# Self-attention: the narrow score parts of both heads share a bank and one maximum

## What is computed

```python
def _L1_attn_ref(x, wq, wk, wv, wo):
    NUM_HEADS = 16
    N, L, E = x.shape
    H, d = NUM_HEADS, E // NUM_HEADS
    q = (x @ wq.T).reshape(N, H, L, d)
    k = (x @ wk.T).reshape(N, H, L, d)
    v = (x @ wv.T).reshape(N, H, L, d)
    scores = jnp.einsum('nhld,nhmd->nhlm', q, k) / jnp.sqrt(jnp.float32(d))
    causal = jnp.tril(jnp.ones((L, L), dtype=bool))
    scores = jnp.where(causal, scores, jnp.float32(-jnp.inf))
    attn = jax.nn.softmax(scores, axis=-1)
    wei = jnp.einsum('nhlm,nhmd->nhld', attn, v).reshape(N, L, H * d)
    return wei @ wo.T
```

## Time and profile before

| | us |
|---|---|
| median of 3 runs (lowest, highest) | 3203.89 (3202.26, 3206.14) |
| the profiled execution, device time | 3204.56 |
| its span, first to last instruction | 3203.0 |
| of it self-attention's tiles, about | 1335 to 2108 |

### The profile page before, as it was taken

One profiled execution on the slowest core, in us unless ns is written; L12 is line 12 of the kernel. 1 busy time (PEld: TensorE's weight loads), 2 busy tenths in 40 slices (PEclk: granted clock), 3 DMA queues, 4 the chain that ended last, 5 costly groups with the idle time before them and its releaser, 6 DMA issues. The chain is left out here.

```text
span 3203.0 us, 41427 instructions
## 1 busy us (share of the span) xinstructions
PE 2843.9 (89%) x14210; PEld 1845.6 (58%) x14210; DVE 2080.0 (65%) x3833; ACT 1471.0 (46%) x2768; POOL 1509.9 (47%) x1192
## 2 busy tenths in 40 slices
PE   6898998998977877899999999978877999999998
PEld 2343343343333664555555555546666888888887
DVE  7899999999998654677777777758863222222221
ACT  5667667666763301366666656545541111111111
POOL 5788788888785553133333333256752111111111
PEclk8999999999999788899999999999888999999999
DMA  7135145145140162212322222110115665556662
GB/s 233 51 108 159 46 116 160 35 125 159 34 136 1 41 211 94 81 42 65 81 63 65 58 50 64 50 59 29 50 63 198 200 203 183 181 181 187 205 199 60
DMA packets 283856, 346.32 MB, mean 108 GB/s; under 512 B 85788, under 2 KB 238552, under 8 KB 283592
## 3 DMA queue, kind: packets, MB, share of 16 engines
q1 hardware_dynamic: 260399, 310.17, 31.3%
q0 software_dynamic: 16704, 27.21, 3.6%
q10 hardware_dynamic: 6544, 6.30, 0.7%
HBM read 234.69 MB, written 107.95 MB: 107 GB/s over the span
## 5 line engine op out<-in xcount | busy, mean ns | idle before, releaser
L542 POOL TENSOR_TENSOR mb_drive<-mb_dtx,mb_b_rep 128x1024 f32<-128x1024 f32 x255 | 597.0, 2355 | 179.9 <-DVE mb_pD L439 87.9
L853 PE MATMUL mb_pY<-mb_hc,ident 128*128 128x512 f32 x1024 | 502.9, 616 | 55.9 <-DVE mb_hc L456 55.5
L1981 DVE TENSOR_REDUCE at_nm_of<-at_pS 128x1 f32<-128x128 f32 (+1 forms) x756 | 401.6, 556 | 135.8 <-PE at_pS L1969 75.8
L3153 POOL DMA_INDIRECT out<-et_y,et_to x71 | 112.0, 1577 | 667.0 <-DVE et_y L3207 411.0
L3197 DVE TENSOR_TENSOR et_mT<-et_silu,et_pU 128x512 f32<-128x512 f32 (+1 forms) x160 | 100.3, 628 | 471.2 <-ACT et_silu L3168 471.1
L3168 ACT ACTIVATE et_silu<-et_pG 128x512 f32<-128x512 f32 (+1 forms) x160 | 87.8, 549 | 658.0 <-PE et_pU L3229 658.0
L853 PEld LDWEIGHTS mb_pY<-mb_hc,ident 128*128 128x128 f32 x1024 | 190.3, 195 | 326.9 <-issue 183.3
L1969 PE MATMUL at_pS<-at_kT,at_qT 128*128 128x128 f32 (+1 forms) x756 | 306.3, 407 | 65.3 <-DVE at_nm_of L1981 53.4
L598 ACT ACTIVATE mb_pD<-mb_dt,mb_a_neg 128x512 f32<-128x512 f32 x384 | 259.6, 688 | 157.3 <-DVE mb_hc L456 146.0
L439 DVE TENSOR_TENSOR_SCAN mb_pD<-mb_pD,mb_drive 128x1024 f32<-128x1024 f32 x128 | 292.7, 2287 | 42.9 <-ACT mb_pD L596 40.2
L445 DVE TENSOR_TENSOR_SCAN mb_pD<-mb_pD,mb_carried,mb_drive 128x512 f32<-128x512 f32 x256 | 314.0, 1271 | 6.8 <-ACT mb_pD L598 6.8
(11 more groups left out here) (491 smaller groups left out, 4984.7 us busy)
## 6 DMA issues: line engine op xcount, KB each, us to landing
t_wg<-in_t_wgT SPq DMA_DIRECT2D x40, 1024.0 KB, 6.3
t_wu<-in_t_wuT SPq DMA_DIRECT2D x40, 1024.0 KB, 8.8
t_wd<-in_t_wdT SPq DMA_DIRECT2D x40, 1024.0 KB, 11.3
mb_b_rep<-mb_rows SPq DMA_DIRECT2D x64, 512.0 KB, 5.6
mb_c_rep<-mb_rows SPq DMA_DIRECT2D x64, 512.0 KB, 4.8
t_h_sorted<-blank SPq DMA_DIRECT2D x6, 4160.0 KB, 20.2
t_h_sorted<-blank SPq DMA_DIRECT2D x18, 1170.0 KB, 6.2
t_h_sorted<-blank SPq DMA_DIRECT2D x12, 1040.0 KB, 5.8
```

Of the source, the lines that this page charges most:

```text
L542: nc.gpsimd.tensor_tensor(drive[G % RINGS][:, :, :], dtx[:, m, :].unsqueeze(1).to_broadcast([P, 2, CH]), b_rep[:, 2 * j:2 * j + 2, :], ALU ...
L853: last = nc.tensor.matmul(pY[:, :], K.ident[:, :], hc[G % RINGS][:, k, :], start=False, stop=(j == PAIRS - 1 and k == 1))
L1981: nc.vector.tensor_reduce(nm_of[t % 2][:, w0 // 512, a, qb:qb + 1], score_bank(t, k)[:, 0:w1 - w0], axis=AX.X, op=ALU.max, negate=True).th ...
```

## The change

A part of at most 256 keys becomes one unit for both sides: TensorE writes side 0 into the first columns of the bank and side 1 behind it, each with its mask, and signals once. VectorE reduces both with one instruction, which views the bank as two rows of keys and writes two maxima per query. Parts of 384 and 512 keys stay one unit per side. This gives 20 units (`NS`), and the groups' sizes become 3, 2, 2 at the head and 3, 2, 2, 2, 2, 2 for the rest. So `extra` has work only in g0 and g6. The same matmuls with the same shapes run as before. Only the grouping, the waits and their places in the order differ.

```diff
-        S_SIZES = [3, 3, 2, 3, 3, 3, 3, 2, 2]
-        S_ORDER = [(n, a) for n in range(NSP) for a in range(2)]
-        NS = len(S_ORDER)
+        S_SIZES = [3, 2, 2, 3, 2, 2, 2, 2, 2]
+        S_UNITS = []
+        for n, (qb, w0, w1) in enumerate(S_PARTS):
+            S_UNITS += [(n, [0, 1])] if w1 - w0 <= 256 else [(n, [0]), (n, [1])]
+        NS = len(S_UNITS)
...
-            last = nc.tensor.matmul(out[:, 0:w1 - w0], qT[b][:, a, h, qb * P:(qb + 1) * P], kT[b][:, a, h, w0:w1],
-                                    start=True, stop=not diag)
-            if diag:
-                last = nc.tensor.matmul(out[:, w1 - w0 - P:w1 - w0], ident_bf[:, :], after[:, :], start=False, stop=True)
+            for x, a in enumerate(sides):
+                last = nc.tensor.matmul(out[:, x * w:(x + 1) * w], qT[b][:, a, h, qb * P:(qb + 1) * P], kT[b][:, a, h, w0:w1],
+                                        start=True, stop=not diag)
+                if diag:
+                    last = nc.tensor.matmul(out[:, (x + 1) * w - P:(x + 1) * w], ident_bf[:, :], after[:, :], start=False, stop=True)
...
-            nc.vector.tensor_reduce(nm_of[t % 2][:, w0 // 512, a, qb:qb + 1], score_bank(t, k)[:, 0:w1 - w0], axis=AX.X,
+            nc.vector.tensor_reduce(nm_of[t % 2][:, w0 // 512, sides[0]:sides[0] + m, qb],
+                                    score_bank(t, k)[:, 0:m * w].rearrange("p (a w) -> p a w", a=m), axis=AX.X,
...
-                if nxt if g < 6 else far:
-                    pe_score(eng, i + ahead, x + ahead, pair, (S_AT[g + 3] if g < 6 else S_AT[g - 6]) + 2)
+                n = g + 3 if g < 6 else g - 6
+                if S_SIZES[n] > 2 and (nxt if g < 6 else far):
+                    pe_score(eng, i + ahead, x + ahead, pair, S_AT[n] + 2)
```

More of the change, by code:

```diff
@@ L1948, in score_bank, with pe_score @@
             return (pS + pE)[k % 4] if t == 0 else pS[k % 2]
-        def pe_score(eng, t, x, pair, k):
-            n, a = S_ORDER[k]
+        def pe_score(eng, t, tile, pair, k):
+            n, sides = S_UNITS[k]
             qb, w0, w1 = S_PARTS[n]
+            w = w1 - w0
             diag = w1 == (qb + 1) * P
-            b, h = x // 2 % 2, x % 2
+            b, h = tile // 2 % 2, tile % 2
             if k == 0 and h == 0:
@@ L1968, in pe_score @@
             out = score_bank(t, k)
-            last = nc.tensor.matmul(out[:, 0:w1 - w0], qT[b][:, a, h, qb * P:(qb + 1) * P], kT[b][:, a, h, w0:w1],
-                                    start=True, stop=not diag)
-            if diag:
-                last = nc.tensor.matmul(out[:, w1 - w0 - P:w1 - w0], ident_bf[:, :], after[:, :], start=False, stop=True)
+            for x, a in enumerate(sides):
[3 more added lines that the diff above has]
+                    last = nc.tensor.matmul(out[:, (x + 1) * w - P:(x + 1) * w], ident_bf[:, :], after[:, :], start=False, stop=True)
             last.then_inc(s_sc, 1)
         def dve_score(eng, t, k):
-            n, a = S_ORDER[k]
+            n, sides = S_UNITS[k]
             qb, w0, w1 = S_PARTS[n]
+            w, m = w1 - w0, len(sides)
             eng.wait_ge(s_sc, t * NS + k + 1)
@@ L2259, in scores @@
                 if nxt if g < 6 else far:
-                    base = S_AT[g + 3] if g < 6 else S_AT[g - 6]
-                    for k in range(base + lo, base + hi):
+                    n = g + 3 if g < 6 else g - 6
+                    base = S_AT[n]
+                    for k in range(base + lo, base + min(hi, S_SIZES[n])):
                         dve_score(eng, i + ahead, k)
```

## The result

The changed kernel takes 3154.75 us in the median (3152.41 to 3156.51, four executions) against 3203.07 us for the kernel before in the same session. The ratio is 0.9847, with a 95% interval of 0.983 to 0.9864: faster by 48 us, where 43 had been forecast.

A forecast was written before the change was run, and what follows sets the result against it. TensorE's stream sets the pace, losing time in pauses for VectorE's reduces. 14 tile pairs x (1.96 + 0.78) = 38.4 us, 42.5 with the other tiles, plus 0.3 at the first: profiled 3204.6 to 3161.7, forecast 3161 us, range 3156 to 3167.

The forecast's parts named there:

- the order for four engines: Hand-written walk through a tile's order, waits and durations; gave 21.34 us odd and 26.15 even for the kernel before.
- The saving on VectorE: Four fewer reduce instructions a tile, likelier 0.3 us of VectorE's time each tile; worth between nothing and 19 us.
- The even tile: Waits of 1.71, 1.37 and 0.5 us removed, 0.50 at v11 and 1.7 through ScalarE given back; net gain 1.96 us.
- The odd tile: Losses of 2.7 us removed in g0 to g4, 2.0 given back; with g6 and uncovered loads, a gain of 0.78 us.
- seven "losses": Odd tile, g0 to g4: seven delays of TensorE's score loads waiting for VectorE's reduces, adding up to 2.7 us.
- (b): Rival: more than the walk, a longer even-tile wait and g4's ScalarE waits go; 0.5 us more a pair, 3153 us; chance 0.12.
- The head: First tile: 20 units instead of 24 in VectorE's chain, saving 0.3 us for the four instructions.
- The maxima's way back: Row transfer of maxima to the next tile: cover falls from 1.4 to 1.5 us to 0.8, costing nothing.
- (a): Rival: ScalarE's chain takes nearly all the even tile's gain, leaving 0.82 us there; 24.5 us in all, 3179; chance 0.17.
- (c): Rival: the maxima come late by 1.2 us, each tile loses 0.4; 12 us less gain, 3173; chance 0.04.
- (d): Rival: waits reappear at the next bank, only 0.3 us of instruction overhead a tile saved; 10 us, 3194; chance 0.03.
- (e): Rival: coarser hand-over of merged units costs 1.6 us a tile; kernel slower by 7 us, 3211; chance 0.04.

The follow-up runs named there:

- e1: Changed kernel's order, but all 24 units keep their own bank, signal and reduce, narrow sides back to back; ratio to the kernel before 0.9958.
- e3: Kernel before, with VectorE reducing the third units of g1 and g3 ahead of the casts of turnings 3 and 7; ratio to before 0.9904.
- e4: Changed kernel, with its third units back in g1 and g3, behind VectorE's casts; ratio to the kernel before 0.9942.
- e6: Changed kernel with the third unit in g2 instead of g0; ratio to the kernel before 0.9835, odd tile 19.90 us.
- e7: Changed kernel with the casts of turning 5 made by VectorE instead of ScalarE; ratio to the kernel before 0.9806, even tile 23.48 us.
- e9: Changed kernel with only 128-key parts sharing a bank, 256-key parts two units again (22 units); one execution, 3166.7 us.
- e10: Changed kernel with the third unit in g2 and turning 5's casts on VectorE; one execution, 3158.2 us, even tile 24.31, odd 19.90.
- e2: Changed kernel with each merged unit reduced by two VectorE instructions, signalled after the second; ratio to the kernel before 0.9843.
- e8: Changed kernel with three useless small DMAs on SyncE ahead of the four carrying the maxima, a 1.32 us delay; one execution, 3185.5 us.

## Why the prediction was right, and where it was off

**The bound.** Right. TensorE's stream set the pace, and its waits for VectorE's reduces were the loss: as they went, the tiles shrank by about what the order for four engines had given, and none of e1, e3, e4, e6, e7, e9 and e10 came out more than 0.3 us a tile from what that order said of it.

**The saving on VectorE.** I left it between 0 and 19 us and put nothing of it into the tiles' sum. e2 shows the lower end: nothing. The two-row reduces cost what I had read from the earlier trace rows, 420 and 693 ns.

**The even tile.** Forecast 24.19, measured 24.23; but the gain was 2.17 us and not 1.96. What was taken away has the size forecast: the steps from load to load at the two pauses shrank from 1.82 to 0.23 us and from 1.61 to 0.11, together 3.09 where 3.08 stood in the sum, and that at the 384-key unit of g3 by 0.59 (0.5). The mis-sized term is what is given back. It was 0.52 us at v11 (0.50 forecast; it is loaded 2.80 us after the odd tile's start, 2.82 forecast), 0.20 + 0.19 at the two E of g4 (0.3), about 0.06 at product 0 (0.15), and at turning 7 only 0.51 us "more than before" (0.75): the wait is 0.78 us now, but 0.27 of it had been there. That makes 1.5 us instead of 1.7. ScalarE works without a gap, and e7 confirms its chain. The 0.27 may also be the 0.25 us by which my order for the tile before was short (26.15 against 26.40); that is not shown.

**The odd tile.** Forecast 20.56, measured 20.35, gain 1.00 and not 0.78. This came near in part by luck, for both sides of my sum were too large. One of the seven "losses" was none. It is the one at the third unit of g2, which follows product 0. The product's matmuls and that load in the kernel before, then the product in the changed one:

```profile
1718.88 1.07 PE L2093 MATMUL at_pO<-at_e,at_v 128*32 128x512 f32 x8
1719.88 0.19 PEld L1969 LDWEIGHTS at_pS<-at_kT,at_qT 128*128 128x128 f32 x1 [0.84 <-DVE at_nm_of L1981]
```

```profile
1698.09 1.06 PE L2099 MATMUL at_pO<-at_e,at_v 128*32 128x512 f32 x8
```

TensorE was busy with the product's matmuls for the whole 0.84 us, and the reduce that the load at 1719.88 needs had ended at 1718.77. Most likely this is what I counted with 0.76 us (1.00 less 0.24). In the same way the 0.84 us of idle time that the table puts down to ScalarE at 1699.08 lies under product 0 and is hardly a loss. Given back were 0.36 us at v9 (0.46 forecast), 0.52 at v11 (0.50), about 0.2 at product 0 (0.55; its load comes 0.71 us behind the one ahead, against 0.50 in the even tile before), and nothing in g4, where the 0.5 us did not appear. So about 1.1 us were given back, not 2.0, and about 2 taken away, not 2.7.

The places of the loads show where the gain arises: the first E of g3 comes 6.31 us after the tile's start in both kernels, and from there to g4's product the tile gains 0.99 us (9.68 to 8.69), where the kernel before had three waits of 0.52, 0.22 and 0.30 us for reduces. In g6, 0.66 us for the first unit (0.68), and none for the second (0.12).

**The sum.** 14 x 2.74 became 14 x 3.17; the median came out at 3154.75, 1.3 us below the forecast's own range and between it and rival (b). My own range, to which I had given 0.60, was missed by that little. (b) gave each pair 0.5 us more and 0.43 were measured, but not by its way: no wait that I had too short went away, and the waits for ScalarE in g4 are not covered in the even tile (0.39 us).

**The head.** Forecast -0.3 us, measured +1.1. VectorE's chain of 20 units did end 0.13 us sooner (from 1337.12 to 1350.05 against 1335.03 to 1348.09), but the first E now waits for the row's DMA:

```profile
1357.00 0.29 PEld L2049 LDWEIGHTS at_pE<-at_qT,at_kT 128*128 128x128 f32 x1 [1.63 <-DMA at_qT<-at_nmT]
```

The load comes 6.95 us after the transposes of the maxima, 5.69 before. In the profiles of all runs that share a bank but e8 that stretch is between 5.5 and 7.1 us, each time with a wait for this DMA of 0.79 to 1.79; in before, e1 and e3 (5.7 to 6.3 us) no wait for it is shown. Why it takes longer at the head, I can't say.

**The maxima's way back.** Right: a cover of 1.49 us before and 0.80 after by e8's distance, where 1.4 to 1.5 and 0.8 had been forecast. In the changed kernel only two loads of an E between 1400 and 2060 us wait for this DMA, 0.8 us in all, so it cost almost nothing in the steady tiles.

**The rivals.** (a), that ScalarE takes nearly all of the even tile's gain, gave a gain of 0.8 us there against 2.17 measured. (c) fell with e8, but for the head, where the first E does wait for the row; (d) fell with the sum. (e) fell too: the merged units are handed over later, and e1 shows that giving each side its own bank in the same place costs 1.16 us in the even tile and 1.06 in the odd one. But a sentence in (e) was too simple. I wrote that the casts' waits "go by the order alone", as if their 3.1 us a pair were safe without the shared bank. They do go (in e1 no score load behind the casts waits more than 0.55 us), yet in e1 the narrow units, back to back, take half of it again, and the even tile gains 1.0 us, not 1.84 as in e3. Nor did the prediction see the other side of it: that in before itself the same waits could be removed by moving two lines. It credited one change with two effects that can be had apart.

**The signs.** All the signs of the profile came out but one. I had expected the wait of score loads for VectorE at about half of 109.5 us, and it fell to 29.9, a bit over a quarter. Part of the old sum was no loss, like the 0.84 us above; in the changed kernel such idle time carries ScalarE's name.

**What stays open.** The stages ahead took 2.1 us more here and the last mixture of experts 5.8 less, in one profile each, with the same code; I take this for chance and have not tested it. The 1.7 us lost between the last tile and that mixture I have not followed.

## What to carry to other kernels

Where two engines hand small units over through two banks, count the hand-overs on the producer's side and look at what stands ahead of each on the consumer's: merging narrow units saves the wait, about 0.25 us for each hand-over taken away in the odd tile here, while the saved instruction is worth nothing. Look first for long instructions of other work that stand between a unit and its hand-over; moving a reduce ahead of two casts brought 28 of 48 us, without any new layout. And before idle time of a load is counted as a loss, look whether TensorE's matmuls still run over it: 0.84 us of idle weight loads lay under a product here. A wait that the change seems to bring may have been there before in part, like turning 7's.

## What the hardware showed beyond that

- A reduce of two rows to two outputs costs no more than one row of the same length: 693 against 687 ns for 512 keys in all, 420 against 422 for 256.
- Two reduces with a signal after the second cost the same time as one in this stage (24.23 and 20.37 us a tile against 24.23 and 20.35), although the line through 286, 422 and 687 ns gives each about 0.15 us of its own.
- The eight matmuls of product 0 (32 weight columns, 512 columns each) take 1.07 us, and the weight load behind them starts 1.00 us after the first of them; the 0.84 us of idle time in the row of weight loads carries the name of a reduce that had ended 1.1 us before.
- A DMA of 8 numbers on each of 128 partitions takes 0.43 us to issue, against 0.67 for each of the four that carry the maxima; and the consumer's load comes 3.88 us after the first of the four begins to be issued (e8, one execution), where the earlier trace rows had given at most 3.9.
